# A fused cross-attention and ternary FFN layer: row transposes moved from TensorE to VectorE and DRAM, and a start-up in another order

## The chip, the cores and the metric

The kernel runs on one core of a Trainium2 chip. The metric is the device time of one launch in microseconds (us). Before the change the median of three runs was 1545.11 us (1544.32 to 1546.74).

## The reference

Input `x` is 32 sequences of 256 rows of 256 numbers, `ctx` is 32 sequences of 77 rows of 256. All is float32. The four attention matrices are 256x256, the ternary FFN matrices (entries -1, 0, 1) are 1024x256, 1024x256, 1024x1024, 1024x1024 and 256x1024, each with a scale per output.

```
def layer(x, ctx):
    q = heads(layernorm(x) @ Wq.T + bq)          # 8 heads of 32
    k, v = heads(ctx @ Wk.T + bk), heads(ctx @ Wv.T + bv)
    p = softmax(q @ k.T / sqrt(32) + causal)     # 256 x 77
    x = x + merge(p @ v) @ Wo.T + bo
    h = silu(tlin(n, w1, s1)) * tlin(n, w2, s2)  # n = layernorm(x), tlin(x, w, s) = (x @ w.T) * s
    h = gelu(tlin(h, h1, s_h1))
    h = gelu(tlin(h, h2, s_h2))
    return x + tlin(h, w3, s3)
```

## The kernel before

**Tiles.** Rows are taken 512 at a time (two sequences), so there are 16 tiles. A loop runs over them: one pass does the FFN of tile `f` and, in between, the attention of tile `f + 1` and the first layernorm and query product of tile `f + 2`. The last two passes stand outside the loop; in pass 14 there is no tile `f + 2`, in pass 15 there is only the FFN.

**The order of the work is written out by hand.** `ORDER` is a list of step names; every engine walks the same list and issues its own part of each step. Within a pass: `L1` (eight products with w1 and w2), `L2`, `L3` (eight each, 16 matmuls in one), `L4` (the output product, two halves). An activation is split into a high part (`a_hi`, rounded to TensorE's fp32r form) and the rest (`a_lo`); both are multiplied, hence two matmuls for each product. Attention steps are put between FFN steps: `S` scores, `MASK`, `MAX`, `SUB`, `EXP`, `SOFT`, `DT` (VectorE transposes probabilities in 32x32 blocks), `MV` (the blocks go to DRAM and come back put together), `PV`, `O` (output projection), `LN2S` and `LN2A` (statistics and application of the second layernorm, giving `xln`), `T2` (`xln` is transposed so that features lie on partitions, then split into `ln2_hi` on ScalarE and `ln2_lo` on VectorE), `LN1S`, `ROWS`, `LN1A` (first layernorm of the tile after; its input comes already transposed as `x_t`, its statistics go through DRAM to be broadcast), `Q`.

**T2 before.** TensorE makes eight 128x128 transposes from `xln` into banks 0 and 1 of `att_banks` (L670), ScalarE copies them to `ln2_hi` (L804), VectorE subtracts (L971). `L1` of the next pass waits for `ln2t_done`. `Q` uses the same banks and waits for `ln2t_done` too.

**The start-up.** `FIRST` is the list of steps before the loop. It does tile 0's attention, and the keys and values of tiles 2 to 15 (`KX`, `VX` on TensorE; `KD` on ScalarE and `VD` on VectorE take the results out of three rotating banks of `ffn_banks`). The 11 weight pieces (1 MB each) are loaded by SyncE's queue; `CHECK` steps look on ScalarE or VectorE at whether they are exact in fp32r, `COUNT` and `FLAG` sum that up, `READ` brings the flag into TensorE's sequencer, which branches on it to one of two versions of the loop. `KEEP` and `SPILL` steps copy weights in place and keys and values to DRAM. Before any of it, TensorE multiplies the identity by itself 20 times (`spin`, L505) while the first loads come in.

**Queues.** All DMAs are issued by SyncE in the order of the list, and a wait there holds back all later issues. `x_in`, `x_t` of the tile after next are loaded in step `CTX`, after `x1_done`.

Of the kernel before, what the change touches and what calls it, by code (L numbers as in the profile page):

```python
# [23 lines left out]
P = 128  # L24
# [7 lines left out]
NQ = TILE // P  # L32
# [10 lines left out]
def column_of(head):  # L43
# [8 lines left out]
ACT_CHECKS = (0, 1, 2, 3, 4, 5, 7)  # L52
DVE_CHECKS = (6, 8, 9, 10)
# [16 lines left out]
def steps(f, a, b):  # L70
# [7 lines left out]
FIRST = [  # L78
# [6 lines left out]
    ("KD", 6, 0), ("VX", 1, 0), ("CHECK", 1, 0), ("O", 0, 0), ("CHECK", 8, 0), ("CHECK", 9, 0), ("CHECK", 2, 0),  # L85
# [20 lines left out]
def build_kernel(nc, x, x_t, ctx_t, ctx_later, w_att, vectors, w1, w2, h1, h2, w3, out):  # L106
# [4 lines left out]
    with ExitStack() as es:  # L111
# [74 lines left out]
        heads_t, _ = put("heads_t", [P, KD, TILE], at=probs_at)  # L186
        x1, _ = put("x1", [P, NQ, D], at=probs_at + 2 * H * TK * 4)
# [28 lines left out]
        tails_dram = [nc.dram_tensor(f"tails_dram{n}", (P, H // 2 * NB * 32), F32, kind="Internal").ap() for n in range(NB)]  # L216
        k_dram = nc.dram_tensor("k_later_dram", (P, HG, LATER), F32, kind="Internal").ap()
# [10 lines left out]
        kv_w_loaded, q_w_loaded, o_w_loaded = sem("kv_w_loaded"), sem("q_w_loaded"), sem("o_w_loaded")  # L228
        vec_loaded, rows_vec_loaded = sem("vec_loaded"), sem("rows_vec_loaded")
# [32 lines left out]
        x_biased, x1_done, x1_kept = sem("x_biased"), sem("x1_done"), sem("x1_kept")  # L262
        t2_ready, ln2hi_done, ln2t_done = sem("t2_ready"), sem("ln2hi_done"), sem("ln2t_done")
# [62 lines left out]
        def _(sp):  # L326
# [115 lines left out]

# [28 lines left out]
        def _(pe):  # L471
# [35 lines left out]
            def one_pass(f, a, b, general):  # L507
                for step, n, t in steps(f, a, b):
                    c0 = chunk_base.get((step, n))
                    if step == "L1":  # L510
# [6 lines left out]
                        if n == 1:  # L517
                            pe.wait_ge(out_scaled, 2 * f + 2)
# [581 lines left out]
```

## Time and profile before

| | |
|---|---|
| median of 3 runs | 1545.11 us (1544.32 to 1546.74) |
| the profiled execution | 1543.65 us |
| its span, first to last instruction | 1541.9 us |
| busy: TensorE, VectorE, ScalarE, GpSimd | 99%, 52%, 45%, 8% |
| one pass on TensorE | 92.8 us |
| first FFN matmul of the loop | 67.77 us after the span's start |
| granted TensorE clock | 1.00 |

The profile is of one execution. "PE" is TensorE's matmuls, "PEld" its weight loads, DVE is VectorE, ACT ScalarE, POOL GpSimd, SP SyncE (which issues the DMAs). A line number is one of the kernel before. In a timeline, a start time is followed by the duration and the instruction; what stands in brackets is the idle time before it and what ended it. Matmuls overlap, so the distance from one start to the next tells more than a duration.

### The profile page before, as it was taken

To read this page: it belongs to the slowest core of one execution; us is meant where nothing else is said; L and a number is where in the kernel's file an instruction comes from. 1 tells how busy PE (TensorE), PEld (TensorE's weight loads), DVE (VectorE), ACT (ScalarE), POOL (GpSimd) and SP (SyncE) were. 2 spreads that over 40 slices of the span, in tenths; PEclk is the share of its full clock that TensorE was granted. 3 is DMA by queue.
4 is the path that set the end of the run, shared out by engine and by line. 5 is a ranking of instruction groups with operands and counts; after the bars stand their busy time and mean duration, and the time that the engine had idled before them with its cause. 6 is when DMAs were issued, how large, how long until landed. Compare 5 with 4: busy or idle time off the path is not lost.

```text
span 1541.9 us, 21318 instructions
## 1 busy us (share of the span) xinstructions
PE 1532.9 (99%) x8422; PEld 1249.0 (81%) x8422; DVE 802.0 (52%) x1276; ACT 697.2 (45%) x1013; POOL 123.1 (8%) x134
## 2 busy tenths in 40 slices
PE   9999999999999999999999999999999999999998
PEld 6787888888888887888888888887888888888887
DVE  6664735547354474644548354474644547354332
ACT  4653534436354453534536354353634536354342
POOL 1001011010100201001010100201001010100000
PEclk9999999999999999999999999999999999999999
DMA  9951020212202121020212202121030211202000
GB/s 377 347 189 50 32 84 27 75 48 65 57 14 77 53 67 49 31 85 27 75 41 64 65 14 75 55 67 49 24 92 27 75 41 64 64 16 68 14 1 15
DMA packets 50529, 106.32 MB, mean 69 GB/s; under 512 B 9026, under 2 KB 24394, under 8 KB 47690
## 3 DMA queue, kind: packets, MB, share of 16 engines
q1 hardware_dynamic: 50506, 106.00, 21.1%
q8 instruction: 16, 0.26, 0.1%
q14 instruction: 7, 0.06, 0.0%
HBM read 61.93 MB, written 32.52 MB: 61 GB/s over the span
## 4 chain that ended last, share of the span: by engine, by line
PE 96%; DMA 1%; SPq 1%; DVE 0%; ACT 0%; issue 0%; ACTq 0%
PE ffn_banks L479 84%; PE att_banks L660 4%; PE att_banks L602 3%; PE att_banks L619 2%; PE att_banks L650 2%; DMA h_bits<-in_h 1%; PE att_banks L670 1%; SPq L370 1%; PE ffn_banks L693 0%; ACT junk L725 0%; SPq L349 0%; PE ffn_banks L685 0%; DVE inexact L861 0%; PE att_banks L590 0%; DVE a_lo L887 0%
## 5 line engine op out<-in xcount | busy, mean ns | idle before, releaser
L479 PE MATMUL ffn_banks<-b_hi,h_sb 128*128 128x512 f32 x1024 | 404.4, 395 | 0.0
L479 PE MATMUL ffn_banks<-b_lo,h_sb 128*128 128x512 f32 x1024 | 399.0, 390 | 0.0
L479 PE MATMUL ffn_banks<-a_hi,h_sb 128*128 128x512 f32 x1024 | 398.3, 389 | 0.0
L479 PE MATMUL ffn_banks<-a_lo,h_sb 128*128 128x512 f32 x1024 | 398.3, 389 | 0.0
L759 ACT ACTIVATE a_f<-ffn_banks,vec 128x512 f32<-128x512 f32 x128 | 88.2, 689 | 367.1 <-PE ffn_banks L479 367.1
L887 DVE TENSOR_TENSOR a_lo<-a_f,a_hi 128x512 fp32r<-128x512 f32 x128 | 94.5, 739 | 298.0 <-ACT a_hi L760 297.9
L479 PEld LDWEIGHTS ffn_banks<-b_hi,h_sb 128*128 128x128 f32 x1024 | 192.3, 188 | 45.1 <-issue 6.2
L479 PEld LDWEIGHTS ffn_banks<-a_hi,h_sb 128*128 128x128 f32 x1024 | 192.2, 188 | 39.9
L479 PEld LDWEIGHTS ffn_banks<-a_lo,h_sb 128*128 128x128 f32 x1024 | 192.2, 188 | 39.9
L479 PEld LDWEIGHTS ffn_banks<-b_lo,h_sb 128*128 128x128 f32 x1024 | 192.3, 188 | 38.9
L479 PE MATMUL ffn_banks<-ln_hi,w_sb 128*128 128x512 f32 x512 | 203.6, 398 | 0.6 <-DVE v_later L915 0.6
L479 PE MATMUL ffn_banks<-ln_lo,w_sb 128*128 128x512 f32 x512 | 200.4, 391 | 0.0
L887 DVE TENSOR_TENSOR b_lo<-b_f,b_hi 128x512 fp32r<-128x512 f32 x128 | 84.6, 679 | 180.2 <-ACT b_hi L760 180.2
L759 ACT ACTIVATE b_f<-ffn_banks,vec 128x512 f32<-128x512 f32 x128 | 88.3, 690 | 193.5 <-PE ffn_banks L479 192.0
L743 ACT ACTIVATE a_f<-ffn_banks,vec 128x512 f32<-128x512 f32 x128 | 88.3, 690 | 163.2 <-PE ffn_banks L479 163.2
L479 PE MATMUL ffn_banks<-w_sb,a_hi 128*128 128x256 f32 x512 | 129.3, 294 | 0.8 <-DVE a_lo L887 0.8
L479 PE MATMUL ffn_banks<-w_sb,a_lo 128*128 128x256 f32 x512 | 123.6, 283 | 0.0
L876 DVE SCALAR_TENSOR_TENSOR a_f<-ffn_banks,vec,a_f 128x512 f32<-128x512 f32 x128 | 95.8, 749 | 52.9 <-PE ffn_banks L479 51.6
L479 PEld LDWEIGHTS ffn_banks<-ln_hi,w_sb 128*128 128x128 f32 x512 | 96.1, 188 | 22.7 <-issue 1.0
L479 PEld LDWEIGHTS ffn_banks<-ln_lo,w_sb 128*128 128x128 f32 x512 | 96.2, 188 | 19.4
L479 PEld LDWEIGHTS ffn_banks<-w_sb,a_hi 128*128 128x128 f32 x512 | 98.2, 192 | 4.7 <-issue 3.3
L479 PEld LDWEIGHTS ffn_banks<-w_sb,a_lo 128*128 128x128 f32 x512 | 98.2, 192 | 3.4 <-issue 3.3
(103 smaller groups left out, 1580.9 us busy)
## 6 DMA issues: line engine op xcount, KB each, us to landing
blocks_dram<-blocks SPq DMA_DIRECT2D x30, 512.0 KB, 3.0
attn_t<-blocks_dram SPq DMA_DIRECT2D x60, 256.0 KB
h_bits<-in_h SPq DMA_DIRECT2D x8, 1024.0 KB, 19.1
h_sb<-h_bits SPq DMA_DIRECT2D x8, 1024.0 KB, 8.5
out<-out_sb SPq DMA_DIRECT2D x32, 256.0 KB, 2.0
x_in<-in_x SPq DMA_DIRECT2D x15, 512.0 KB, 3.6
ln_t<-in_x_t SPq DMA_DIRECT2D x14, 512.0 KB, 4.4
ln_rows<-ln_rows_dram SPq DMA_DIRECT2D x14, 512.0 KB, 4.0
```

The lines of the kernel that those rows point to most:

```text
L370: sp.dma_start(pieces[c][1], pieces[c][0]).then_inc(piece_loaded[c], 16)
L479: mm = nc.tensor.matmul(psum, left, right, start=(k == 0 and part == 0), stop=(k == rows - 1 and part == 1))
L602: mm = nc.tensor.matmul(ab[:, m, :], wq_sb[:, k, m * P:(m + 1) * P], ln1_t[:, k, :], start=(k == 0), stop=(k == KD - 1))
L619: mm = nc.tensor.matmul(ab[:, h, at:at + TK], q_t[rows, g, tokens], k_t[rows, g, n * TK:(n + 1) * TK], start=True, stop=True)
L650: mm = nc.tensor.matmul(ab[HD * h:HD * (h + 1), bank, g * TQ:(g + 1) * TQ], v_sb[:, n, (4 * g + h) * HD:(4 * g + h + 1) * HD], probs_t, st ...
L660: mm = nc.tensor.matmul(ab[:, 2 + j // 2, (j % 2) * D:(j % 2 + 1) * D], heads_t[:, k, j * P:(j + 1) * P], wo_sb[:, k, :], start=(k == 0), ...
L670: mm = nc.tensor.transpose(ab[:, k, j * P:(j + 1) * P], xln[:, j, k * P:(k + 1) * P], id32[:])
L743: nc.scalar.activation(a_f32[:, n, :], fb[:, 2 * (n % 2), :], ACT.Silu, scale=s1_sb[:, n:n + 1]).then_inc(silu_done, 1)
L759: nc.scalar.activation(f32[:, n, :], fb[:, n % 4, :], ACT.Gelu, scale=scale[:, n:n + 1])
L876: nc.vector.scalar_tensor_tensor(out=a_f32[:, n, :], in0=fb[:, 2 * (n % 2) + 1, :], scalar=s2_sb[:, n:n + 1], in1=a_f32[:, n, :], op0=ALU. ...
L887: nc.vector.tensor_tensor(lo[:, n, :], f32[:, n, :], hi[:, n, :].bitcast(F32), ALU.subtract).then_inc(done, 1)
```

## The change

There are two parts.

*The transposition of a tile's rows in the loop (T2).* TensorE no longer takes part. VectorE transposes `xln` in 32x32 blocks (two instructions) into `row_blocks`, a buffer that lies where `heads_t` does. Step `XW` writes it to DRAM, step `XR` reads it back with four DMAs so that the blocks lie in their places. ScalarE and VectorE then make `ln2_hi` and `ln2_lo` from it, in two instructions each. In `ORDER`, `LN1S` now stands ahead of `LN2A`, and `T2` behind `L3, 7`. `Q` waits for `x1_done` instead of `ln2t_done`. The first tile's T2, in the start-up, stays on TensorE.

*The start-up.* `FIRST` begins with `KX` 0 and 1 and `VX` 0 and 1, ahead of tile 0's own keys, transposes and queries. Their operands are loaded first (a `w_att` slice and part 0 of `ctx_later`), and the combined loads of two weight matrices and of the vectors are split. `spin` goes from 20 to 14. Weight checks are spread differently and piece 10 goes from VectorE to ScalarE. `L1, 0` of the loop waits for all `VX` results but the last, `L1, 1` for the last.

```diff
-ACT_CHECKS = (0, 1, 2, 3, 4, 5, 7)
-DVE_CHECKS = (6, 8, 9, 10)
+ACT_CHECKS = (0, 1, 2, 3, 4, 5, 7, 10)
+DVE_CHECKS = (6, 8, 9)
 ORDER = [
...
-    ("L3", 0), ("L3", 1), ("O", 0), ("CTX", 0), ("LN2S", 0), ("L3", 2), ("LN2A", 0), ("LN1S", 0), ("L3", 3), ("ROWS", 0), ("L3", 4),
-    ("L3", 5), ("LN1A", 0), ("L3", 6), ("T2", 0), ("L3", 7), ("Q", 0), ("L4", 0),
+    ("L3", 0), ("L3", 1), ("O", 0), ("CTX", 0), ("LN2S", 0), ("L3", 2), ("LN1S", 0), ("LN2A", 0), ("XW", 0), ("ROWS", 0), ("XR", 0), ("L3", 3), ("L3", 4),
+    ("L3", 5), ("LN1A", 0), ("L3", 6), ("L3", 7), ("T2", 0), ("Q", 0), ("L4", 0),
...
 FIRST = [
+    ("KX", 0, 0), ("KX", 1, 0), ("KD", 0, 0), ("KD", 1, 0), ("VX", 0, 0), ("VD", 0, 0), ("VX", 1, 0), ("VD", 1, 0),
     ("K", 0, 0), ("T1", 0, 0), ("V", 0, 0), ("LN1S", 0, 1), ("Q", 0, 0), ("XLN", 0, 1),
...
+        row_blocks, _ = put("row_blocks", [P, 4, KD, P], at=probs_at)
...
# SyncE
+                    if step == "XW":
+                        sp.wait_ge(rows_blocked, t)
+                        sp.dma_start(row_blocks_dram, row_blocks[:]).then_inc(row_blocks_out, 16)
+                    if step == "XR":
+                        sp.wait_ge(row_blocks_out, 16 * t)
+                        for b_ in range(4):
+                            src = row_blocks_dram[:, b_].rearrange("(r f) k i -> f r (k i)", r=4)
+                            dst = row_blocks[32 * b_:32 * b_ + 32].rearrange("f r k i -> f r (k i)")
+                            sp.dma_start(dst, src).then_inc(row_blocks_back, 16)
...
+            sp.dma_start(w_att_sb[:, 1], w_att[:, 1]).then_inc(k_w_loaded, 16)
+            load_later_ctx(0)
             sp.dma_start(x_in[:], x_tiles[0]).then_inc(x_loaded, 16)
+            sp.dma_start(vec[:, 0:n_small], vectors[:, 0:n_small]).then_inc(vec_loaded, 16)
+            sp.dma_start(w_att_sb[:, 2], w_att[:, 2]).then_inc(v_w_loaded, 16)
+            sp.dma_start(vec[:, n_small:n_small + D], vectors[:, n_small:n_small + D]).then_inc(bv_loaded, 16)
             load_ctx(0)
-            sp.dma_start(w_att_sb[:, 1:3], w_att[:, 1:3]).then_inc(kv_w_loaded, 16)
-            sp.dma_start(vec[:, 0:n_small + D], vectors[:, 0:n_small + D]).then_inc(vec_loaded, 16)
             sp.dma_start(w_att_sb[:, 0], w_att[:, 0]).then_inc(q_w_loaded, 16)
-            load_later_ctx(0)
             sp.dma_start(x1_keep[:], x_tiles[1]).then_inc(x2_loaded, 16)
...
# TensorE
+                            pe.wait_ge(vx_done, (NCH + 1) // 2 - 1)
+                        if n == 1:
                             pe.wait_ge(vx_done, (NCH + 1) // 2)
-                        if n == 1:
                             pe.wait_ge(out_scaled, 2 * f + 2)
...
-                            pe.wait_ge(ln2t_done, t)
+                            pe.wait_ge(x1_done, t)
...
-                    if step == "T2":
+                    if step == "T2" and f is None:
                         pe.wait_ge(ln_ready[1], t + 1)
-                        if f is None:
-                            pe.wait_ge(q_done, 2)
+                        pe.wait_ge(q_done, 2)
...
-            spin(20)
-            pe.wait_ge(kv_w_loaded, 16)
+            spin(14)
+            pe.wait_ge(k_w_loaded, 16)
...
# ScalarE
                     if step == "T2":
-                        act.wait_ge(t2_ready, t + 1)
-                        nc.scalar.copy(ln2_hi[:], ab[:, 0:2, :]).then_inc(ln2hi_done, 1)
...
+                            act.wait_ge(row_blocks_back, 64 * t)
+                            for k in range(KD):
+                                op = nc.scalar.copy(ln2_hi[:, k].rearrange("p (j r q) -> p j r q", r=4, j=NQ),
+                                                    row_blocks[:, :, k].rearrange("p r (j q) -> p j r q", j=NQ))
...
# VectorE
                         ln_apply(x1, 1, t)
+                        if f is not None:
+                            dve.wait_ge(ln_ready[1], t + 1)
+                            for k in range(KD):
+                                op = nc.vector.transpose(row_blocks[:, :, k, :],
+                                                         xln[:, :, k * P:(k + 1) * P].rearrange("p j (b f) -> p b j f", b=4))
+                            op.then_inc(rows_blocked, 1)
...
+                            for k in range(KD):
+                                low, high = (x[:, k].rearrange("p (j r q) -> p j r q", r=4, j=NQ) for x in (ln2_lo, ln2_hi))
+                                op = nc.vector.tensor_tensor(low, row_blocks[:, :, k].rearrange("p r (j q) -> p j r q", j=NQ),
+                                                             high.bitcast(F32), ALU.subtract)
```

What this makes of VectorE's queue in the loop, from the output projection's sum (`x_88`, `x_89` are `x1`) to the last FFN product's rest (`a_lo`). Before:

```order
L961 TENSOR_TENSOR x_88<-att_banks,x_in 128x1024
L817 BN_STATS st_98<-x_88 128x6 x4
L820 MEMSET spare 128x1
L822 BN_AGGR mv_100<-st_98 128x2 x4
L887 TENSOR_TENSOR a_lo<-a_f_63,a_hi 128x512
L829 TENSOR_SCALAR xln<-x_88,mv_100,rstd_103 128x256 x4
L977 REGISTER_ALU
L817 BN_STATS st_97<-x_in 128x6 x4
L819 REGISTER_ALU
L820 MEMSET spare 128x1
L822 BN_AGGR mv_99<-st_97 128x2 x4
L887 TENSOR_TENSOR a_lo<-a_f_63,a_hi 128x512 x3
```

And now, in the same place:

```order
L909 TENSOR_TENSOR a_lo<-a_f_63,a_hi 128x512
L1012 REGISTER_ALU
L839 BN_STATS st_98<-x_in 128x6 x4
L841 REGISTER_ALU
L842 MEMSET spare 128x1
L844 BN_AGGR mv_100<-st_98 128x2 x4
L851 TENSOR_SCALAR xln<-x_89,mv_101,rstd_104 128x256 x4
L994 STREAM_TRANSPOSE row_blocks<-xln 128x4x128 x2
L909 TENSOR_TENSOR a_lo<-a_f_63,a_hi 128x512 x3
```

The statistics of the newly loaded `x_in` now stand ahead of the normalization of `x1`, and two transposes follow it; all of that is ahead of the next three `a_lo`.

SyncE's DMAs of the same stretch, from the load of the tile after next. Before:

```order
L328 DMA x_in<-in_x 128x1024
L331 DMA ln_t<-in_x_t 128x1024
L335 REGISTER_ALU
L336 DMA ln_rows_dram<-ln_stat 128x2x4
L339 ISA
L341 DMA ln_rows<-ln_rows_dram 128x1024
```

And now:

```order
L331 DMA x_in<-in_x 128x1024
L334 DMA ln_t<-in_x_t 128x1024
L338 REGISTER_ALU
L339 DMA ln_rows_dram<-ln_stat 128x2x4
L424 REGISTER_ALU
L425 DMA row_blocks_dram<-row_blocks 128x1024
L342 ISA
L344 DMA ln_rows<-ln_rows_dram 128x1024
L427 REGISTER_ALU
L431 DMA row_blocks<-row_blocks_dram 32x4x256 x4
```

The write of the blocks stands ahead of the broadcast of the statistics (`ln_rows`), the four reads behind it.

TensorE's queue at the end of the start-up, from tile 0's transposes to the branch (`v_later` products are `ffn_banks<-w_att_sb,c_later`). Before:

```order
L670 MATMUL att_banks<-id_91,xln 128x128 x8
L685 MATMUL ffn_banks<-c_later,w_att_sb 128x512 x2
L685 MATMUL ffn_banks<-c_later,w_att_sb 128x108 x4
L693 MATMUL ffn_banks<-w_att_sb,c_later 128x256 x16
L700 MATMUL ffn_banks<-ones,inexact_row 1x1
L693 MATMUL ffn_banks<-w_att_sb,c_later 128x256 x4
L703 TENSOR_LOAD flag
L703 ISA x2
L693 MATMUL ffn_banks<-w_att_sb,c_later 108x256 x2
L711 COMPARE_AND_BRANCH
```

And now:

```order
L684 MATMUL att_banks<-id_92,xln 128x128 x8
L708 MATMUL ffn_banks<-w_att_sb,c_later 128x256 x8
L715 MATMUL ffn_banks<-ones,inexact_row 1x1
L708 MATMUL ffn_banks<-w_att_sb,c_later 108x256 x2
L718 TENSOR_LOAD flag
L718 ISA x2
L726 COMPARE_AND_BRANCH
```

Less is left to do behind the transposes, and the flag is now read behind the last product, directly ahead of the branch.

## Rows read from the trace of the kernel before

**Rows 1.** The page: busy time, share of the span, instructions by engine.

```profile
PE 1532.9 (99%) x8422; PEld 1249.0 (81%) x8422; DVE 802.0 (52%) x1276; ACT 697.2 (45%) x1013; POOL 123.1 (8%) x134
```

**Rows 2.** Chain that ended last, pass 5: start us, us, what.

```profile
590.91 18.16 PE ffn_banks L479 x80
609.06 0.87 PE att_banks L670 x8
...
613.58 3.43 PE att_banks L602 x8
617.01 9.51 PE ffn_banks L479 x72
```

**Rows 3.** Timeline of VectorE, the same pass: start, us, instruction [idle before].

```profile
590.94 1.23 DVE L961 TENSOR_TENSOR x<-att_banks,x_in 128x1024 f32<-128x1024 f32 x1 [1.46 <-PE att_banks L660]
...
596.49 1.38 DVE L829 TENSOR_SCALAR xln<-x,mv,rstd 128x256 f32<-128x256 f32 x4
597.79 1.40 DVE L817 BATCH_NORM_STATS2 st<-x_in 128x6 f32<-128x256 f32 x4
...
606.76 0.69 DVE L887 TENSOR_TENSOR a_lo<-a_f,a_hi 128x512 fp32r<-128x512 f32 x1 [2.50 <-ACT a_hi L760]
607.59 1.23 DVE L840 TENSOR_TENSOR ln_t<-ln_t,ln_rows 128x1024 f32<-128x1024 f32 x1
```

**Rows 4.** Timeline of SyncE's DMA issues, the same pass.

```profile
592.33 0.37 SPq L328 DMA_DIRECT2D x_in<-in_x  x1
...
601.38 0.38 SPq L336 DMA_DIRECT2D ln_rows_dram<-ln_stat  x1
603.89 0.34 SPq L341 DMA_DIRECT2D ln_rows<-ln_rows_dram  x1
```

**Rows 5.** Groups by line: shapes xcount | busy us, mean ns | idle before.

```profile
L754 ACT CAST a_hi<-a_f 128x512 fp32r<-128x512 f32 x128 | 78.5, 613 | 7.9 <-DVE a_f L876 7.9
...
L946 DVE STREAM_TRANSPOSE blocks<-probs 128x512 f32<-128x512 f32 x60 | 39.2, 691 | 2.4
```

**Rows 6.** DMA issues over the span: count, KB each, median us to landing.

```profile
blocks_dram<-blocks SPq DMA_DIRECT2D x30, 512.0 KB, 3.0
...
h_bits<-in_h SPq DMA_DIRECT2D x8, 1024.0 KB, 19.1
...
x_in<-in_x SPq DMA_DIRECT2D x15, 512.0 KB, 3.6
```

**Rows 7.** Timeline of TensorE in the start-up.

```profile
8.32 1.22 PE L584 MATMUL att_banks<-ctx_sb,w_att_sb 128*128 128x154 f32 x8
...
30.54 1.97 PE L635 MATMUL att_banks<-id,probs 128*77 128x128 f32 x16 [1.23 <-DVE probs L939]
...
38.15 1.93 PE L650 MATMUL att_banks<-attn_t,v_sb 77*32 77x256 f32 x32 [0.45 <-DVE attn_t L953]
...
64.02 0.19 PE L700 MATMUL ffn_banks<-ones,inexact_row 128*1 128x1 f32 x2 [0.22 <-DVE inexact_row L867]
...
67.77 0.47 PE L479 MATMUL ffn_banks<-ln_hi,w_sb 128*128 128x512 f32 x1 [0.61 <-DVE v_later L915]
```

**Rows 8.** Busy time by window, line L505 (spin) alone: window, us, PE, PEld, PEclk, DMA.

```profile
5.00:6.00 1.00, 1.00 (x6) 1.00 (x6) 1.00 0.70 181
6.00:7.00 1.00, 1.00 (x11) 1.00 (x10) 1.00 0.78 232
```

**Rows 9.** DMA issues from 1.16 to 3.5 us: count, KB each, us to landing.

```profile
w_att_sb<-in_w_att SPq DMA_DIRECT2D x1, 512.0 KB, 6.1
...
ctx_sb<-in_ctx_t SPq DMA_DIRECT2D x1, 154.0 KB, 3.4
```

**Rows 10.** Timeline of SyncE at the start: the third issue.

```profile
1.66 0.43 SPq L445 DMA_DIRECT2D w_att_sb<-in_w_att  x1
```

**Rows 11.** Timeline of TensorE's weight loads at the end of the start-up.

```profile
66.05 0.70 PEld L693 LDWEIGHTS ffn_banks<-w_att_sb,c_later 128*108 128x108 f32 x4 [0.32 <-issue]
67.74 0.19 PEld L479 LDWEIGHTS ffn_banks<-ln_hi,w_sb 128*128 128x128 f32 x1 [1.00 <-issue]
```

More of the change, by code:

```diff
@@ L78 @@
 FIRST = [
[1 row of a table added]
     ("K", 0, 0), ("T1", 0, 0), ("V", 0, 0), ("LN1S", 0, 1), ("Q", 0, 0), ("XLN", 0, 1),
[5 rows of a table removed]
-    ("KD", 6, 0), ("VX", 1, 0), ("CHECK", 1, 0), ("O", 0, 0), ("CHECK", 8, 0), ("CHECK", 9, 0), ("CHECK", 2, 0),
[5 rows of a table removed]
[5 rows of a table added]
+    ("CHECK", 6, 0), ("VX", 5, 0), ("VD", 5, 0), ("CHECK", 4, 0), ("CHECK", 5, 0), ("CHECK", 7, 0), ("CHECK", 8, 0), ("O", 0, 0),
+    ("Q", 0, 1), ("CHECK", 10, 0), ("ADD", 0, 0), ("LN2S", 0, 0), ("K", 0, 1), ("V", 0, 1),
+    ("LN2A", 0, 0), ("BIAS", 0, 1), ("VADD", 0, 1), ("CHECK", 9, 0), ("T2", 0, 0), ("COUNT", 0, 0),
+    ("VX", 6, 0), ("VD", 6, 0), ("VX", 7, 0), ("VD", 7, 0), ("FLAG", 0, 0), ("VX", 8, 0), ("READ", 0, 0), ("VD", 8, 0),
     ("KEEP", 0, 0), ("SPILL", 0, 0), ("KEEP", 1, 0), ("SPILL", 1, 0), ("KEEP", 2, 0),
@@ L216, in build_kernel @@
         tails_dram = [nc.dram_tensor(f"tails_dram{n}", (P, H // 2 * NB * 32), F32, kind="Internal").ap() for n in range(NB)]
+        row_blocks_dram = nc.dram_tensor("row_blocks_dram", (P, 4, KD, P), F32, kind="Internal").ap()
         k_dram = nc.dram_tensor("k_later_dram", (P, HG, LATER), F32, kind="Internal").ap()
@@ L227, in build_kernel @@
         x_loaded, x2_loaded, ctx_loaded, stored = sem("x_loaded"), sem("x2_loaded"), sem("ctx_loaded"), sem("stored")
[L228 to L229 removed]
+        k_w_loaded, v_w_loaded = sem("k_w_loaded"), sem("v_w_loaded")
+        q_w_loaded, o_w_loaded = sem("q_w_loaded"), sem("o_w_loaded")
+        vec_loaded, bv_loaded, rows_vec_loaded = sem("vec_loaded"), sem("bv_loaded"), sem("rows_vec_loaded")
         piece_loaded = [sem(f"piece_loaded{i}") for i in range(11)]
@@ L451, in _ @@
             load_piece(0)
+            load_later_ctx(2)
+            load_later_ctx(3)
             load_piece(1)
-            load_later_ctx(2)
             sp.dma_start(vec[:, n_small + D:], vectors[:, n_small + D:]).then_inc(rows_vec_loaded, 16)
+            load_later_ctx(4)
             sp.dma_start(w_att_sb[:, 3], w_att[:, 3]).then_inc(o_w_loaded, 16)
             load_piece(2)
-            load_later_ctx(3)
-            load_later_ctx(4)
             for c in range(3, NP):
@@ L688, in one_pass @@
                     if step == "VX":
+                        pe.wait_ge(v_w_loaded, 16)
                         pe.wait_ge(later_loaded[2 * P * n // GROUP], 16)
@@ L802, in one_pass @@
                     if step == "T2":
-                        act.wait_ge(t2_ready, t + 1)
-                        nc.scalar.copy(ln2_hi[:], ab[:, 0:2, :]).then_inc(ln2hi_done, 1)
+                        if f is None:
+                            act.wait_ge(t2_ready, 1)
+                            op = nc.scalar.copy(ln2_hi[:], ab[:, 0:2, :])
+                        else:
+                            act.wait_ge(row_blocks_back, 64 * t)
+                            for k in range(KD):
+                                op = nc.scalar.copy(ln2_hi[:, k].rearrange("p (j r q) -> p j r q", r=4, j=NQ),
+                                                    row_blocks[:, :, k].rearrange("p r (j q) -> p j r q", j=NQ))
+                        op.then_inc(ln2hi_done, 1)
             act.wait_ge(dve_consts, 1)
@@ L968, in one_pass @@
                         ln_apply(x1, 1, t)
+                        if f is not None:
[4 more added lines that the diff above has]
+                            op.then_inc(rows_blocked, 1)
                     if step == "T2":
                         dve.wait_ge(ln2hi_done, t + 1)
-                        nc.vector.tensor_tensor(ln2_lo[:], ab[:, 0:2, :], ln2_hi[:].bitcast(F32), ALU.subtract).then_inc(ln2t_done, 1)
+                        if f is None:
+                            op = nc.vector.tensor_tensor(ln2_lo[:], ab[:, 0:2, :], ln2_hi[:].bitcast(F32), ALU.subtract)
+                        else:
+                            for k in range(KD):
+                                low, high = (x[:, k].rearrange("p (j r q) -> p j r q", r=4, j=NQ) for x in (ln2_lo, ln2_hi))
+                                op = nc.vector.tensor_tensor(low, row_blocks[:, :, k].rearrange("p r (j q) -> p j r q", j=NQ),
+                                                             high.bitcast(F32), ALU.subtract)
+                        op.then_inc(ln2t_done, 1)
                     if step == "LN1S":
@@ L996, in _ @@
             dve.wait_ge(vec_loaded, 16)
+            dve.wait_ge(bv_loaded, 16)
             dve.wait_ge(out_ready, 2)
```

1 line of the change is left out of this document (added), and 15 rows, old and new, of the table FIRST.

## The prediction

> **What bounds the kernel now.** I read the page first: TensorE is busy 99% of the span, the other engines at most 52% [rows 1]. A busy share alone proves little, so I went to the chain of waits for one pass [rows 2]. All of it is TensorE's work, back to back: from 590.91 us 80 FFN matmuls, eight transposes of 0.87 us, the query product at 613.58, then 72 FFN matmuls. Passes repeat every 92.8 us (the table ahead). So in the loop an instruction taken from TensorE is worth its whole time, provided that what replaces it is ready when TensorE gets there. The third view, TensorE's timeline of the start-up, is another matter: the loop begins at 67.77 us, the first useful matmul at 8.32, and there are real gaps, of 1.23, 0.45, 0.22 and 0.61 us [rows 7]. There the work's order and the loads count.
>
> **Part 1: the transposes in the loop.** Removed: eight TensorE transposes in each of 15 passes (T2 of tiles 1 to 15; tile 0's stays). Each set takes 0.87 us of the chain [rows 2]: 15 x 0.87 = 13.05 us. Nothing is added to TensorE.
>
> What is added lies elsewhere, and I follow it through pass 5 to see whether it is in time. Without T2, `L3, 7` ends 0.87 earlier than before, at 612.7; the query product runs from there to 616.1, and L4 after it; the next pass's `L1, 0` begins where before it began: 617.01 + 9.51 - 2.1 (its last eight of 72 matmuls) = 624.4, less 0.87, 623.5 [rows 2].
> - VectorE: `x1` is summed from 590.94 to 592.2 [rows 3]. `LN1S` now stands first and needs `x_in`, issued at 592.33 [rows 4] and landing 3.6 later [rows 6], 596.0. The `a_lo` ahead of it ends at 596.5, so `LN1S` takes 1.40 + 0.5 from 596.5 to 598.4, the normalization 1.38 to 599.8 [rows 3], and two block transposes at 0.65 (60 in 39.2 us) end at 601.1 [rows 5]. This delays the next `a_lo` by under 2 us, but `a_lo` is first read in L4, and its engine has pauses of 2.5 us between two of them [rows 3].
> - SyncE: the 512 KB write is issued at 601.2. The probabilities' blocks are of the same size and come from the same kind of instruction: 3.0 us [rows 6], so 604.2. The four reads are issued from then to about 605.9. No row has their landing. Nearest are the single 512 KB loads: 3.0 and 3.6 us [rows 6], and 3.7 for `ln_rows` (603.89 to 607.59) [rows 3, 4]. Farthest is 19.1, a 1 MB load in a full queue at the start [rows 6]. The queue is all but empty here, so I take 4.0 behind the last issue, 609.9, and 1 us more for the broadcast of `ln_rows` in flight beside them.
> - ScalarE reaches T2 behind the activations of `L3, 7`, about 614.0. The blocks have been back for 3 us. Two casts of 0.61 [rows 5] end at 615.2, two subtractions at about 0.69 (the 606.76 row of [rows 3]) at 616.6. `L1, 0` wants them at 623.5, so 6.9 us are spare. If the reads were late, 10 us could pass behind 610.9 before TensorE waits.
>
> The tightest place is another: `ln_rows`. Its DMA is now queued on SyncE behind the wait for the block transposes, and `LN1A`, then `Q` on TensorE, wait for it. Before it was issued at 603.89, 2.5 behind the write of the statistics at 601.38 [rows 4], and `LN1A` began at 607.59 [rows 3], 3.7 later, which is its landing. Now `LN1S` ends 1.2 us earlier, so the statistics are written at 600.2; the block write at 601.2 passes in between without holding anything, and the broadcast goes out at 602.7, 1.2 earlier than before. If the 512 KB of blocks in front delay it by up to 1.5, it lands at 606.5 to 608. `LN1A` is 2 x 1.23 behind that [rows 3], 610.5 at worst; the query product asks at 612.7. Spare: 2.2 us.
>
> Value taken: 13.05. Its ends: 0 if all is given back at `Q` in every pass, and a little over 13 if the changeover to and from the transposes goes too.
>
> The Trainium skill has a rule that speaks against such a path. "VectorE: DVE Perf Modes", section "The three transpose paths", says that VectorE transposes 32x32 blocks only, and that a plain DMA which does the rest with strides can be 19 times slower than the hardware's transposing DMA when the innermost stride at the destination is large. No row here shows a transposing DMA. Each piece moved here is a run of 1 KB, which the rule does not mean. If it held all the same, its result would be rival D; as an estimate by its figure, 19 x 3.6 = 68 us for the reads, of which 54 would be waited for in each of 15 passes, some 2340 us in all.
>
> **Part 2: the start-up.** Three things move.
> - *The beginning.* `spin` ends earlier. Spins run at 6 records in the us before 6.0 and 11 in the one after [rows 8], two records a spin, so a spin takes 0.33 and then 0.18. Fourteen of them, started at 1.6, end at about 6.3 (13 by 6.0, one after); I take 6.4. Then `KX, 0` needs 768 KB: a 256 KB weight slice and 512 KB of context. Before, 666 KB had landed at 1.2 + 3.4 = 4.6, and 1178 KB at 1.66 + 6.1 = 7.8 [rows 9, 10]; 768 KB lies between, about 5.3. So TensorE starts at 6.4 instead of 8.32 [rows 7]: 1.9 gained, with 0.5 (load at 7.8) and 2.5 as ends. Behind it come 6.9 us of key and value products, and by then (13.3) tile 0's layernorm, whose input has moved from first to third load, is ready at about 13.0. That is close, and part of the uncertainty.
> - *The middle.* One more product step, worth about 1.7, now stands between the scores and the first transposes of probabilities, so the gap of 1.23 goes; the weight check in front of the attention copy on VectorE is moved, so the 0.45 goes as well [rows 7]. New: `KX, 6` waits for a bank that ScalarE empties behind `EXP`, 0.3. Together 1.68 - 0.3 = 1.4 gained.
> - *The end.* Before: FLAG waits 0.22, and between the last weight load of the `VX` products (66.75) and the first of the loop lies 1.00 [rows 7, 11], most of it a wait for the last `VD`. Now that wait is gone, but VectorE has a check, tile 0's T2, `COUNT` and two `VD` (0.69 each) queued in front of the flag's cast, and the flag is read behind the last product, with the branch directly after. The cost of the read is seen only as 0.32 of pause behind it, and the branch was hidden in the 1.00; so read and branch cost between 0.3 and 1.3. I count 0.6 for FLAG and 1.4 for the rest, against 1.2 before: a loss of 0.8. With about 0.5 of small pauses that vanish: -0.3.
>
> Sum of part 2: 1.9 + 1.4 - 0.3 = 3.0, with ends of 0 (the load late, the flag dear) and 5.
>
> On the clock: the granted clock is shown as 1.00 in both windows, though the spins run at half the pace in the earlier one [rows 8]. With fewer spins more useful work could fall into the slower stretch. "TensorE: Matmul & The Clock Gate", section "Part 1: The HAM clock gate (the "warmup" mystery)", of the Trainium skill says the clock is at half rate by default and that activity releases it, which agrees with the step in [rows 8]; by it a pause between spins and `KX, 0` could keep the 6.9 us of first products at half pace. I leave that to the range: 6.9 us lost would turn part 2 into a loss of 4.
>
> **Total.** 13.05 + 3.0 = 16.05. The profiled execution took 1543.65 us (span 1541.9 and 1.75 around it), so 1527.6 for it. The median of the runs lies 1.46 above; I carry that over: 1545.11 - 16.05 = 1529.06, forecast 1529.0.
>
> **The rivals.**
> - A, the forecast: both parts work, gain 14 to 20, 1525 to 1531.
> - B, the start-up gives nothing or loses: tile 0's layernorm is late by its load, or the flag holds the branch. For it: the loads at the start are the only stretch before 67.77 where TensorE has no stock of work. Against it: the gaps in [rows 7]. Gain 9 to 13: 1532 to 1536.
> - C, the transposes are gone from TensorE but `Q` waits for `ln_rows`: the margin is 2.2 us. Should the broadcast be 3.1 late, 0.87 is given back in each of 14 passes; only part 2 is left: about 1542.
> - D, slower: the reads of the blocks. ScalarE's queue holds the query's bias and the next pass's SiLU behind T2. It decides when the reads land over 14 us behind their issue (4 taken and 10 spare). Each us beyond costs 15. At the slowest landing in the trace, 19.1 us [rows 6], a pass would wait 5.1, and the time would be 1529 + 77 = 1606; at 16 us it would be 1559. Against it: the attention blocks come back in the same way and the chain shows no wait for them, nor for anything else between 590.91 and 626.5 [rows 2].
> - E, nothing changes because another engine takes the lead. VectorE gets 1.3 + 0.2 a pass more, at 52%: no.
>
> **Chances.** A 0.83, B 0.09, C 0.04 (all but its end still "within"), D 0.02, rest 0.02. The range: A, with the other cases until no more than 0.2 is left out: 1524.5 to 1534. A measurement tells 0.2%, about 3.1 us, from no change. A and B are faster by more; C is about even between faster and same; D is slower. So faster 0.94, same 0.03, slower 0.03.
>
> **What would show it.** No `att_banks<-id,xln` transposes in the loop, passes 0.87 shorter (91.9), no wait on TensorE at `Q` and `L1, 0`: part 1 right. A TensorE wait ahead of `Q` with `ln_t` as its releaser: C. ScalarE idle ahead of `ln_hi` with `row_blocks` DMAs as its end, growing past 10 us: D. The loop's first matmul at 64.8 or less: part 2 right; at 67 or later: B, and then TensorE's first `KX` or the transposes of tile 0 should stand behind a DMA or a layernorm. I am wrong altogether if TensorE's FFN matmuls, 0.23 us from start to start, change their pace.

## The result

The changed kernel takes 1529.9 us (median of four runs, 1528.8 to 1530.9); the kernel before, measured beside it, 1545.1. The ratio is 0.990, 95% interval 0.9883 to 0.9917. Four further runs of it gave 1530.4 against 1545.7, ratio 0.9898 (0.9881 to 0.9914). The forecast was 1529.0, range 1524.5 to 1534.

The profiled execution took 1530.78 us, its span 1529.0. First the page, then the chain that ended last, in pass 5; they answer to [rows 1, 2].

```profile
PE 1518.3 (99%) x8290; PEld 1236.4 (81%) x8290; DVE 834.7 (55%) x1320; ACT 698.9 (46%) x1030; POOL 123.9 (8%) x134
```

```profile
585.00 21.77 PE ffn_banks L493 x96
606.78 3.43 PE att_banks L617 x8
610.21 9.51 PE ffn_banks L493 x72
619.72 1.06 PE att_banks L634 x32
```

The eight transposes of 0.87 us are gone: 96 FFN matmuls run through to the query product, and nothing is waited for there or at the next pass's `L1, 0`. Passes repeat every 91.88 us, where they took 92.78.

**Where the time went.** The last stretch of TensorE before the outputs stands in the chain as 50 matmuls of 6.26 us:

```profile
1516.68 6.26 PE ffn_banks L493 x50
```

In the trace of before the same 50 begin at 1531.58. TensorE is thus 14.90 us ahead: 1.37 from the start-up (the loop's first matmul at 66.40 for 67.77) and 15 x 0.90 = 13.5 from the passes. Of this the span shows only 12.9, since from the start of those matmuls to the end of the span 10.3 us passed before and 12.3 now. That is scatter of an execution: in thirteen traces with the same end the stretch lasts 10.3 to 12.5 us. The 2.0 us between these two lie in the very last write (`out<-out_sb`), which landed 2.1 us behind its issue in the trace of before and 4.2 in that of after. The medians, 15.2 apart, agree with TensorE's 14.9.

**The loop's new path.** VectorE, SyncE's DMA issues and ScalarE in pass 5, answering to [rows 3, 4]:

```profile
590.59 1.40 DVE L839 BATCH_NORM_STATS2 st<-x_in 128x6 f32<-128x256 f32 x4
...
592.32 1.35 DVE L851 TENSOR_SCALAR xln<-x,mv,rstd 128x256 f32<-128x256 f32 x4
593.71 1.31 DVE L994 STREAM_TRANSPOSE row_blocks<-xln 128x512 f32<-128x512 f32 x2
...
601.47 1.22 DVE L862 TENSOR_TENSOR ln_t<-ln_t,ln_rows 128x1024 f32<-128x1024 f32 x1
602.72 1.23 DVE L864 TENSOR_TENSOR ln_t<-ln_t,ln_rows 128x1024 f32<-128x1024 f32 x1
```

```profile
595.04 0.34 SPq L425 DMA_DIRECT2D row_blocks_dram<-row_blocks  x1
596.58 0.32 SPq L344 DMA_DIRECT2D ln_rows<-ln_rows_dram  x1
599.14 1.75 SPq L431 DMA_DIRECT2D row_blocks<-row_blocks_dram  x4
```

```profile
607.97 1.14 ACT L824 CAST ln_hi<-row_blocks 128x512 fp32r<-128x512 f32 x2
```

The blocks are written from 595.04, read from 599.14, and back at 603.8. ScalarE comes to them at 607.97 without a wait, some 4 us later. `ln_t` is done at 603.95, and `Q` begins at 606.78: 2.8 us spare at the tightest place, 2.2 forecast. The DMA issues of the page give the landings (count, KB each, median us):

```profile
row_blocks_dram<-row_blocks SPq DMA_DIRECT2D x15, 512.0 KB, 3.9
row_blocks<-row_blocks_dram SPq DMA_DIRECT2D x60, 128.0 KB, 3.0
```

**The start-up.** TensorE's timeline at the beginning and at the end (its weight load in the last fence), answering to [rows 7, 11]:

```profile
1.64 6.29 PE L519 MATMUL ffn_banks<-id 128*128 128x128 f32 x28 [1.64 <-POOL id L1083]
7.76 1.45 PE L699 MATMUL ffn_banks<-c_later,w_att_sb 128*128 128x512 f32 x3
...
66.40 0.47 PE L493 MATMUL ffn_banks<-ln_hi,w_sb 128*128 128x512 f32 x1 [2.03 <-issue]
```

```profile
63.07 0.09 PEld L715 LDWEIGHTS ffn_banks<-ones,inexact_row 128*1 128x1 f32 x2 [0.46 <-DVE inexact_row L889]
...
66.37 0.19 PEld L493 LDWEIGHTS ffn_banks<-ln_hi,w_sb 128*128 128x128 f32 x1 [2.42 <-issue]
```

The spins (L519) last until 7.9, so the first product starts at 7.76 and not at 6.4. And in front of the loop TensorE stands still for 2.03 us, its weight loads for 2.42, where before they stood for 1.00. The two gaps of the middle, 1.23 and 0.45, are gone. From TensorE's first product to the loop 58.64 us pass, where 59.45 passed before: of the 1.37 us that the loop begins earlier, 0.56 are gained ahead of the first product and 0.81 behind it.

**What the pace of the spins is.** The whole stretch of 14 spins runs at one pace, 6.12 us from 1.64 to 7.76, or 0.44 a spin. In the trace of before a spin takes about as long at first and 0.22 to 0.23 later. The change of pace has a sign in the traces that the windows don't print: the record of the granted clock begins only when it happens, at 6.10 us in before and at 7.74 in after, and for a stretch without a record the windows show 1.00. So a PEclk of 1.00 at the very start says nothing; the distance between matmuls does. In all fourteen traces the pace of the matmuls agrees with where that record begins, and it begins at 4.7 to 9.6 us, now here and now there for one and the same order of work.

### The profile page after: what moved, and what is told of

It reads as the page before. It is cut to its first block, busy times and chain, and to the rows that moved or that the text cites. A ratio compares the mean times of both kernels' runs of the same rounds, so it can differ in the third digit from the quotient of the medians.

```text
span 1529.0 us, 21246 instructions
## 1 busy us (share of the span) xinstructions
PE 1518.3 (99%) x8290; PEld 1236.4 (81%) x8290; DVE 834.7 (55%) x1320; ACT 698.9 (46%) x1030; POOL 123.9 (8%) x134
## 4 chain that ended last, share of the span: by engine, by line
PE 99%; DVE 0%; issue 0%; ACT 0%; POOL 0%; ACTq 0%; POOLq 0%; DVEq 0%
PE ffn_banks L493 85%; PE att_banks L675 4%; PE att_banks L617 4%; PE att_banks L634 2%; PE att_banks L665 2%; PE ffn_banks L699 1%; PE ffn_banks L708 1%; PE ffn_banks L519 0%; PE att_banks L650 0%; PE att_banks L605 0%; DVE inexact L883 0%; PE att_banks L599 0%; PE att_banks L591 0%; DVE a_lo L909 0%; ACT a_f L774 0%
## 5 line engine op out<-in xcount | busy, mean ns | idle before, releaser
L909 DVE TENSOR_TENSOR a_lo<-a_f,a_hi 128x512 fp32r<-128x512 f32 x128 | 109.6, 856 | 273.7 <-ACT a_hi L775 272.3
```

The costliest lines, as they stand in the source:

```text
L909: nc.vector.tensor_tensor(lo[:, n, :], f32[:, n, :], hi[:, n, :].bitcast(F32), ALU.subtract).then_inc(done, 1)
```

## The experiments

**Each part alone.** Two kernels divide the change. `loop_only` keeps `FIRST`, the loads, the checks and `spin(20)` of before; `start_only` keeps the loop's T2 on TensorE.

```diff
# loop_only: ORDER and T2 as changed
-            spin(14)
-            pe.wait_ge(k_w_loaded, 16)
+            spin(20)
+            pe.wait_ge(kv_w_loaded, 16)
# start_only: FIRST and loads as changed, ORDER and T2 of before
-            spin(20)
-            pe.wait_ge(kv_w_loaded, 16)
+            spin(14)
+            pe.wait_ge(k_w_loaded, 16)
```

> The changed loop with the start-up of before (order, loads, 20 spins, checks). My account: the loop is worth 15 x 0.90 = 13.5 us by itself, so about 1531.6 us, passes of 91.9 us, the first FFN matmul of the loop still at 67.8 us. Rival (the start-up gave the gain and the loop only part): over 1535 us, or passes longer than 92.2 us.

> The start-up of after with the loop of before. My account: the loop's first FFN matmul at 66.4 us (64.6 if the spins run at the faster pace early, as the changed kernel's shorter runs suggest), passes 92.8 us, so 1.4 to 3.2 us faster than before, 1542 to 1544 us. Rival (the start-up is worth the 3.0 us of the forecast when the loop does not disturb it): first FFN matmul at 64.8 us in the profile with TensorE's first product at 6.4 us.

Measured beside 1545.75: `loop_only` 1531.8, ratio 0.9914 (0.9897 to 0.993), passes 91.88, loop from 67.87. `start_only` 1543.1 (ten runs, 1542.0 to 1546.5), ratio 0.9987 (0.9977 to 0.9998), passes 92.78, loop from 65.78. So part 1 is worth 14.0 by medians (13.5 by the passes) and part 2 2.6 with a spread of its own. Added up the medians give 16.6, 1.4 more than the whole change brought, which is within that spread; the ratios multiply to 0.990, the ratio of the whole.

**Fewer spins.** If the spins hold the first product, six of them leave the load as the limit.

```diff
-            spin(14)
+            spin(6)
```

> After with 6 spins instead of 14. If the spins are what TensorE does until the first operands are there and nothing more, the first product starts when part 0 of the context lands, about 6.1 us instead of 7.76, the loop starts up to 1.7 us earlier (64.7), and the time is about 1528.3 us. If work before some moment near 7.5 us runs at half pace whatever it is, the first products take up that time: they are longer by about what was saved, and the loop starts 0.8 to 1.0 us earlier at most. If fewer spins put the change of pace off, the first products run at half pace for long and the loop starts later than 66.4.

1531.3, ratio 0.9917 (0.99 to 0.9933), where 1528.3 was expected: nothing gained. The first product did start at 6.20 and the loop at 65.00, 1.4 earlier. TensorE's timeline, and the windows of busy time (us, PE, PEclk, DMA) at the loop's start:

```profile
1.64 2.93 PE L519 MATMUL ffn_banks<-id 128*128 128x128 f32 x12 [1.64 <-POOL id L1083]
6.20 3.24 PE L699 MATMUL ffn_banks<-c_later,w_att_sb 128*128 128x512 f32 x7 [1.63 <-DMA c_later<-in_ctx_later]
...
65.00 0.47 PE L493 MATMUL ffn_banks<-ln_hi,w_sb 128*128 128x512 f32 x1 [2.12 <-issue]
```

```profile
66.00:68.00 2.00, 2.00 (x13) 0.56 1.03 380
68.00:70.00 2.00, 2.00 (x33) 0.50 1.05 336
70.00:72.00 2.00, 2.00 (x6) 0.50 1.04 342
72.00:74.00 2.00, 2.00 (x8) 0.73 1.05 352
```

Behind the pause of 2.12 us the granted clock fell to the lower of its two levels, 0.50. From the loop's first matmul to the query product of pass 0 it took 84.1 us, where the changed kernel took 81.0 (66.40 to 147.38): 3.1 lost, more than the 1.4 gained. The eight first products ran at the full pace here (3.67 us): the record of the granted clock begins at 4.80, while TensorE waited for them.

**The flag early.** The check of piece 9, `COUNT`, `FLAG` and `READ` move ahead: `T2` and `VX, 7` now lie between `FLAG` and `READ`, and `VX, 8` between `READ` and the branch.

```diff
-    ("Q", 0, 1), ("CHECK", 10, 0), ("ADD", 0, 0), ("LN2S", 0, 0), ("K", 0, 1), ("V", 0, 1),
-    ("LN2A", 0, 0), ("BIAS", 0, 1), ("VADD", 0, 1), ("CHECK", 9, 0), ("T2", 0, 0), ("COUNT", 0, 0),
-    ("VX", 6, 0), ("VD", 6, 0), ("VX", 7, 0), ("VD", 7, 0), ("FLAG", 0, 0), ("VX", 8, 0), ("READ", 0, 0), ("VD", 8, 0),
+    ("Q", 0, 1), ("CHECK", 10, 0), ("ADD", 0, 0), ("LN2S", 0, 0), ("CHECK", 9, 0), ("K", 0, 1), ("V", 0, 1),
+    ("LN2A", 0, 0), ("BIAS", 0, 1), ("VADD", 0, 1), ("COUNT", 0, 0), ("VX", 6, 0), ("FLAG", 0, 0), ("VD", 6, 0), ("T2", 0, 0),
+    ("VX", 7, 0), ("READ", 0, 0), ("VD", 7, 0), ("VX", 8, 0), ("VD", 8, 0),
```

> After with the check of piece 9 ahead of the second layernorm's application, COUNT behind the values' bias, and FLAG and READ one product step earlier (FLAG, T2, VX 7, READ, VX 8). If the 2.03 us of pause ahead of the loop's first FFN matmul are the reading of the flag and the branch, both behind the last product, the read now hides behind VX 7 and VX 8, about 1.0 us of branch stays, and the loop starts near 64.6 (1.8 earlier): about 1528 us. Rival (the branch alone, or the fetch of the loop's first instructions, takes the 2 us): the pause stays at 2 us and the loop starts within 0.3 of 66.4.

1527.1 (1525.7 to 1528.4), ratio 0.9886 (0.987 to 0.9903). From the first product to the loop it took 56.80 us instead of 58.64, and the pause of 2.03 became one of 0.46, which VectorE ends and not the branch:

```profile
63.52 0.47 PE L493 MATMUL ffn_banks<-ln_hi,w_sb 128*128 128x512 f32 x1 [0.46 <-DVE v_later L937]
```

Of the 1.84 us 1.57 are this pause; the other 0.27 lie ahead of it, where the order of the work was changed as well.

**The flag ahead of the last product.** This one asks what reading the flag costs by itself.

```diff
-    ... ("FLAG", 0, 0), ("VX", 8, 0), ("READ", 0, 0), ("VD", 8, 0),
+    ... ("FLAG", 0, 0), ("READ", 0, 0), ("VX", 8, 0), ("VD", 8, 0),
```

> After with the flag read ahead of the last product of the start-up (VX 8) instead of behind it. Tells the read from the branch: the pause ahead of VX 8 is cast plus read, the pause ahead of the loop's first FFN matmul is the branch. If the read itself costs about 1 us and the branch about 1 us, VX 8 starts near 65.3 and the loop 1.0 us behind its end, 66.9: 0.5 us later than in after. If the branch is all of it, VX 8 starts at 64.5 and the pause ahead of the loop stays 2 us.

1532.4 in one run. VectorE's cast of the flag, and the product behind the read:

```profile
63.94 0.14 DVE L893 CAST flag<-ffn_banks 1x1 int32<-1x1 f32 x1
```

```profile
65.88 2.01 PE L708 MATMUL ffn_banks<-w_att_sb,c_later 128*108 128x256 f32 x4 [2.81 <-issue]
```

From the cast's end at 64.08 to the product 1.8 us pass: that is the read. The product began 0.6 us later than expected, since the read is dearer than the 1 us that was taken for it. The branch hardly shows here: the loop's first weight load follows the last one after 0.12 us, with four matmuls at half pace ahead of it. In the changed kernel 2.1 us pass from the cast's end at 64.27 to the loop at 66.40; that leaves about 0.3 for the branch, by subtraction, if the read takes as long there. And here, too, the granted clock fell, to 0.50 in the window from 66 to 68.

**Later blocks.** Rival D is tested by writing the rows to DRAM several times before they are read; `delay4` and `delay7` have 4 and 7 in place of 2.

```diff
                     if step == "XR":
-                        sp.wait_ge(row_blocks_out, 16 * t)
+                        for again in range(2):
+                            sp.wait_ge(row_blocks_out, 16 * (3 * (t - 1) + again + 1))
+                            sp.dma_start(row_blocks_dram, row_blocks[:]).then_inc(row_blocks_out, 16)
+                        sp.wait_ge(row_blocks_out, 16 * 3 * t)
```

> After with the write of the blocks to DRAM made two more times, each behind the landing of the one before, ahead of the reads: the blocks come back about 8.5 us later, near 611.5 where the changed kernel has them near 603. If the loop's margin is what the forecast says (the next pass wants them at about 615, TensorE needs them 2.5 us later), ScalarE waits 3 to 4 us ahead of ln_hi, TensorE does not wait, passes stay 91.9 us and the time within 1 us of after's. If ScalarE's wait is passed on at once (query bias behind it), passes grow by over 1 us, 15 us and more in all.

> The same with four more writes: about 17 us later, near 620. With the margin of the forecast TensorE's first FFN matmul of a pass (617.7 in the changed kernel) waits until about 622.5, 4 to 5 us a pass, 60 to 80 us in all, about 1600 us. If nothing waits, the blocks are not what that matmul waits for, and the margin argument was empty.

> In each pass the blocks of the transposed rows are written to DRAM seven times more before they are read back; nothing else is changed. With four more writes the reads were issued at 610.1 us of pass 5, the cast to ln_hi began at 614.3, and TensorE lost only about 0.1 us a pass. The extra writes took 2.9 us each, so with three more the reads are issued at about 618.8 and the cast begins at about 623.0; it, its partner and the subtractions end near 625.3, while the next pass's first product wants them at 617.7. Theory (the margin is used up by the fourth extra write, and beyond it each us is paid once in every pass): a wait of 7.5 to 9 us in each of 15 passes, 1640 to 1665 us in all. Rival (another reserve remains, since ScalarE and VectorE can catch up and only L1 of a pass is held): under 4 us a pass, 1590 or less.

Each is one run. `delay2`: 1529.7, passes 91.88, nothing lost; ScalarE waited 0.9 us a pass and not 3 to 4, for the same reason as in the next run. `delay4`: 1528.5, and my expectation was wrong: no wait of microseconds, because an extra write took 3.1 us (four of them from 597.86 to 610.09) and not 4.1. ScalarE's cast shows the delay, and TensorE's chain how little came of it:

```profile
614.31 1.14 ACT L827 CAST ln_hi<-row_blocks 128x512 fp32r<-128x512 f32 x2 [7.11 <-DMA row_blocks<-row_blocks_dram]
```

```profile
599.78 6.12 PE ffn_banks L496 x27
605.90 3.43 PE att_banks L620 x8
```

ScalarE waits 7.11 us, and a pass is longer by nothing to 0.11: this is the edge. `delay7`: 1672.6, more than the 1640 to 1665 expected. The chain in pass 5 now goes through the writes, and TensorE's timeline shows the wait at `L1, 0` of the next pass:

```profile
643.84 4.05 DMA row_blocks_dram<-row_blocks
647.88 0.02 issue
647.90 2.97 DMA row_blocks_dram<-row_blocks
650.87 0.02 issue
650.88 2.59 DMA row_blocks_dram<-row_blocks
```

```profile
673.39 0.80 PE L496 MATMUL ffn_banks<-ln_hi,w_sb 128*128 128x512 f32 x1 [6.72 <-DVE ln_lo L1007]
```

The waits sum to 102.1 us, 6.8 in each of 15 passes, but the kernel lost 142.7 against the changed one, 9.5 a pass. The remaining 2.7 are the clock. Windows of TensorE's busy time around that wait:

```profile
668.00:670.00 2.00, 0.00 (x0) 0.89 0.84 227
670.00:672.00 2.00, 0.00 (x0) 0.50 0.00 0
672.00:674.00 2.00, 0.61 (x2) 0.50 0.00 0
674.00:676.00 2.00, 2.00 (x6) 0.50 0.00 0
676.00:678.00 2.00, 2.00 (x36) 0.90 0.53 201
```

The clock fell to 0.50 during the pause and rose again only after 676; the first eight FFN matmuls took 3.48 us instead of eight times 0.23. Over the whole trace the granted clock falls once for each of the 15 waits, for 126 us together (the mean granted clock is 0.962). For 44 of them TensorE stood still; in the other 82 it worked at half pace, which costs 41 us. Waits and clock together are 143 us, the whole loss.

**The broadcast behind the reads.** Rival C: `ROWS` behind `XR` makes `ln_rows` later.

```diff
-    ... ("XW", 0), ("ROWS", 0), ("XR", 0), ...
+    ... ("XW", 0), ("XR", 0), ("ROWS", 0), ...
```

> After with ROWS behind XR: the broadcast of the first layernorm's statistics is queued on SyncE behind the four reads. The forecast called this the tightest margin (2.2 us). The broadcast goes out near 601 instead of 596.6, lands near 605.2, LN1A ends at 607.8 where the query product wants it at 606.8: about 1 us of wait on TensorE in each of 14 passes, 12 to 18 us more, about 1544 us. If the margin is larger than I think, no wait and 1530.

1532.7 in one run. VectorE and TensorE:

```profile
604.22 1.23 DVE L862 TENSOR_TENSOR ln_t<-ln_t,ln_rows 128x1024 f32<-128x1024 f32 x1 [2.65 <-DMA ln_rows<-ln_rows_dram]
```

```profile
606.79 3.67 PE att_banks L617 x8
```

`ln_t` is done at 606.70 and the query product takes 3.67 instead of 3.43: the margin is just crossed, 0.24 is paid in this pass. Other passes pay nothing to 1.1, and from the loop's start to the last pass it is 3.4 us more than in the changed kernel. A loss, but smaller than the 12 to 18 us expected.

This trace settles something else. With the broadcast out of the way the write of the blocks lands after 3.0 us, as the forecast had it, and not after 3.9:

```profile
row_blocks_dram<-row_blocks SPq DMA_DIRECT2D x15, 512.0 KB, 3.0
```

So the 0.9 us is what the broadcast costs the write when both are in flight.

**The best version again, and six spins with it.** Four runs each, on one chip with the changed kernel unaltered. `early_spin6` is `early_flag` with `spin(6)`.

> The version with the flag written and read two product steps earlier (14 spins), the same kernel as early_flag, beside the changed kernel on one chip in five rounds. If its gain of 2.8 us in the single comparison (1527.1 against 1529.9) is real, of which the earlier start of the loop accounts for 1.8 and a beginning 1.0 earlier for the rest, it stays 1.8 to 3.0 us below the changed kernel. Rival (the first runs fell on a favourable chip): within 0.8 us of it.

> The changed kernel unaltered, in five rounds beside the early flag on the same chip: 1529.9 us, between 1528.8 and 1531.

> The version with the flag written and read two product steps earlier, and besides that 6 spins instead of 14. Six spins alone brought the first product to 6.20 us, and the loop to 65.00, but there the granted clock fell to half behind a pause of 2.12 us ahead of the loop, and the gain was lost. With the flag early that pause is 0.85 us. Theory (the fall of the clock comes from the long pause together with little work before it, at the branch): here the clock stays at 1.00, the first product starts at 6.2 (6.7 with 14 spins), the loop at 63.0, and the time is 0.5 us below that of the early flag alone, 1526.6. Rival (too few spins leave the clock unsettled, whatever the branch): the granted clock falls again somewhere in the first 75 us, and the time is 1528.5 or more.

| | us, median | lowest to highest | ratio to before |
|---|---|---|---|
| changed kernel | 1530.4 | 1528.5 to 1531.2 | 0.9898 (0.9881 to 0.9914) |
| flag early | 1527.1 | 1526.4 to 1528.2 | 0.9881 (0.9864 to 0.9897) |
| flag early, 6 spins | 1529.4 | 1528.7 to 1530.2 | 0.9897 (0.988 to 0.9913) |

The intervals of the ratios overlap, but all four runs of the early flag lie below all four of the changed kernel, as in the first runs (1525.7 to 1528.4, where the changed kernel had 1528.8 to 1530.9). It is the fastest version, by about 3 us: 1.84 from the earlier start of the loop, and part of the rest from a fall of the granted clock that it is spared, as the next trace shows.

The unaltered kernel gave the most telling trace, since it is a second execution of the same code. Its start and the loop's beginning, then its windows from 64 us:

```profile
1.64 4.85 PE L519 MATMUL ffn_banks<-id 128*128 128x128 f32 x28 [1.64 <-POOL id L1083]
...
65.12 0.47 PE L493 MATMUL ffn_banks<-ln_hi,w_sb 128*128 128x512 f32 x1 [2.18 <-issue]
```

```profile
64.00:66.00 2.00, 0.88 (x4) 1.00 0.98 407
66.00:68.00 2.00, 2.00 (x10) 0.54 1.03 380
68.00:70.00 2.00, 2.00 (x33) 0.60 1.05 339
```

The same 14 spins took 4.85 us here and 6.29 there, because the clock rose at 4.73 here and at 7.74 there; first product at 6.33, close to my 6.4. And behind the same pause the clock fell here and did not there: 82.55 us from the loop's start to the query product of pass 0 instead of 80.98, which gives back 1.57 of the start.

In `early_spin6` I was wrong: its four runs are all slower than those of the early flag alone, by 2.3 us in the median. The rival had the time right (1528.5 or more) and the reason wrong: the granted clock does not fall later, it comes later. Its record begins at 9.64 us.

```profile
6.02 5.47 PE L699 MATMUL ffn_banks<-c_later,w_att_sb 128*128 128x512 f32 x8 [1.45 <-DMA c_later<-in_ctx_later]
```

Eight products take 5.47 us instead of 3.60. Here the slow pace, which the spins otherwise absorb, lasted into useful work; in `spin6` it did not (from 6.20 the same eight took 3.67). In this execution the loop starts at 64.70, where it started at 63.52 and 64.59 in the two with 14 spins, so the start-up explains that nothing was gained; why all four runs are slower by about 2 us stays open. Whether fewer spins make the late clock likelier can't be told from two traces.

## Why the prediction was right, and where not

- *The loop, 13.05.* Right, and 0.45 under: 13.5 by the passes. A pass lost 0.90 and not 0.87, the changeover to and from the transposes with it. `loop_only` shows it alone.
- *The blocks in time.* Right. The write landed after 3.9 us (3.0 taken), the reads after 3.0 (4.0 taken). The forecast had added 1 us to the reads for the broadcast beside them; it was the write that paid it (`rows_late`). The point where D decides was right: by its working the blocks must be back 2.6 us before the next pass's `L1, 0`, which begins at 617.72, so at 615.1; `delay4`, which is at the edge, begins its cast at 614.31 in a pass that lies 0.9 us earlier (`Q` at 605.90 for 606.78), so at 615.2. The price beyond, 15 us for each microsecond, was too low, though it is what the waits alone come to: from the first write to the cast 20.1 us pass in `delay4` (594.17 to 614.31) and 27.0 in `delay7` (643.84 to 670.87), and for these 6.9 us 144 are lost, 21 for each. The half clock after every pause was missing from the sum.
- *The 19-fold rule for strided transposes* (the Trainium skill, "VectorE: DVE Perf Modes", section "The three transpose paths"). It did not apply, as argued: the four reads of 128 KB land in 3.0 us (median of 60), not in 68.
- *The margin at* `Q`. 2.8 us for 2.2. `rows_late` crosses it and loses, so C was a real rival and its place right.
- *The beginning, 1.9.* This step failed. "Spins run at 6 records in the us before 6.0 and 11 in the one after [rows 8], two records a spin, so a spin takes 0.33 and then 0.18." A window counts every record that touches it: for before, the eight windows from 1 to 9 us sum to 54, and there are 40. At the slow pace a spin takes 0.44 (14 of them in the trace of after). With it the same rows give (6.0 - 1.64) / 0.44 = 9.9 slow spins, and 4.1 at about 0.23, an end at 6.9 (0.23, since the other 10.1 of the 20 spins of before fill the 2.32 us from 6.0 to the first product). That is where it came in two executions whose clock rose at the same place as in before (7.0 in `start_only` and `rows_late`). In ten traces with 14 spins the first product starts at 6.33 to 7.77, 7.1 on average: 1.2 gained, not 1.9, and in the profiled execution, whose clock rose 1.6 us later, 0.56.
- *The scatter of it* was missing altogether. The Trainium skill, "TensorE: Matmul & The Clock Gate", section "Part 1: The HAM clock gate (the "warmup" mystery)", warns that the number of slow matmuls at a start differs from run to run of one kernel. The traces agree: 4.85 to 6.33 us for the same 28 records, with the record of the granted clock beginning at 4.73 to 7.81 us. I had cited the section for another point and put a pause there as a risk; the risk was at the other end of the start-up, behind the flag.
- *The middle, 1.4.* Right as far as it can be told: the gaps, 1.68 together, are gone, and no new one of 0.1 us or more has come.
- *The end, -0.3.* Failed: TensorE's two pauses there, 0.83 together before, became one of 2.03, a loss of 1.2. "The cost of the read is seen only as 0.32 of pause behind it, and the branch was hidden in the 1.00; so read and branch cost between 0.3 and 1.3." The read alone takes 1.8 us behind the cast, outside that range (`read_first`), and `early_flag`, which hides it, shortens the pause by 1.57. Before, the read stood ahead of the last product, in a pause of 0.32, and most of it was hidden; an idle time in front of an instruction gives no upper bound for what the sequencer did meanwhile.
- *The sum.* Part 2 was forecast at 3.0 and brought 1.37 in the profiled execution, 2.6 by the medians of `start_only`. From first product to loop 58.6 to 58.8 us pass in each of seven traces, so the mean first product of 7.1 puts the loop at 65.9, 1.9 ahead of before. In two of eight traces with a pause of 2.0 to 2.2 the clock fell behind it. The mean granted clock, which is known for every run, says the same of the spread: of the ten runs of `start_only` the three at 0.997 took 1545.5 to 1546.5 us and the seven at 0.999 or 1.000 took 1542.0 to 1543.8. Of 25 runs of kernels with that pause seven lie at 0.997 or 0.998, of the 12 runs with the early flag none. Where in such a run the clock fell is known only for the profiled ones.

The total came out 1 us from the forecast because 0.45 too little in the loop stood against 1 to 1.6 too much in the start-up; that it came so close is luck in part.

## What to carry to other kernels

Work can be taken off the bounding engine by sending it through idle ones and DRAM, if the distance from the last write to the first reader is counted on every queue that it passes; here there were about 11 us to spare in one place (from the landing at 603.8 to 615.1) and under 3 in another, and the smaller one decides what else may be queued there. A value that steers a branch is to be written early enough that a pause for its read falls behind work. Do not read a rate from window counts without checking that the counts sum to the total. The pace of the first microseconds is told by the distance between matmuls, and a start-up is priced from more than one execution of it.

## What the hardware showed that was not expected

- A flag read into TensorE's sequencer costs 1.8 us from the write that it waits for to the next matmul.
- A pause of 2.0 to 2.2 us on TensorE was followed in two of eight executions by a fall of the granted clock to half, for which 1.6 and 3.1 us were paid; the one of 2.81 and that of 6.72 were followed by it too, the three of 0.46 never. A wait of that length can cost more than its own time: in `delay7` 102 us of waits cost 143.
- The granted clock of TensorE rose 4.7 to 7.8 us after the start of the span in thirteen executions and at 9.6 in one with 6 spins and a pause behind them; until then matmuls ran at half pace, while the windows print 1.00.
- A write of 512 KB took 3.9 us with another DMA of 512 KB in flight beside it, 3.0 without it (medians of 15), and 2.6 when it was repeated at once (median of 105).
- The last write of 256 KB landed 2.1 to 4.3 us behind its issue from one execution to another, so that spans of two traces can differ by 2 us with TensorE's work the same.
